# Cross-attention scores: float32 products in 32-row strips instead of stacked bf16 parts

## What is computed

```python
qh = layernorm(x).reshape(B, 8, 8, 256); kh = vh = ctx.reshape(B, 8, 8, 256)
qk = jnp.einsum('bhdq,bhdl->bhql', qh, kh) * 8 ** -0.5
sm = jax.nn.softmax(qk, axis=-1)
ret = jnp.einsum('bhql,bhdl->bhdq', sm, vh).reshape(B, 64, 256)
x = x + gamma * ret
# feed-forward on layernorm(x); bit_linear rounds its input to 8 bits per row, its weights to -1, 0, 1
h = silu(bit_linear(x, w_gate)) * bit_linear(x, w_up)
h = rms_norm(h, ln_weight)
x = x + bit_linear(h, w_down)
```

## Time and profile before

| what | before |
|---|---|
| time, median of 3 runs | 245.23 us (244.26 to 247.96) |
| span of the profiled execution | 248.6 us |
| PE busy, matrix products | 178.4 us (72%), 1370 records |
| DVE busy | 151.6 us (61%) |
| ACT busy | 140.9 us (57%) |
| POOL busy | 107.3 us (43%) |
| mean granted clock of PE | 0.89 of full |
| DMA | 19.95 MB in 15871 packets |

### The profile page before, as it was taken

How to read it: one execution, slowest core, us unless ns; L and a number is a source line. 1 busy time by engine, 2 the same in 40 slices (tenths; PEclk the granted TensorE clock), 3 DMA queues, 4 the chain that set the end, 5 groups by cost and what they waited for, 6 DMA issues and landing times.

```text
span 248.6 us, 4308 instructions
## 1 busy us (share of the span) xinstructions
PE 178.4 (72%) x1370; PEld 103.8 (42%) x1378; DVE 151.6 (61%) x282; ACT 140.9 (57%) x286; POOL 107.3 (43%) x282
## 2 busy tenths in 40 slices
PE   0006331972988958994999799589979998893793
PEld 0002111540666624662466366245745664441432
DVE  2105840563297974985666989736886769436273
ACT  4110000893466845973568599447856587975432
POOL 3630310406624544734652586436435226626240
PEclk9999999996599997997569999965995699999689
DMA  3599599348201450253026314601540000000000
GB/s 100 139 142 261 126 177 313 115 121 154 63 1 37 118 107 0 56 149 77 1 67 141 75 26 116 135 9 34 142 105 0 5 3 22 7 21 0 22 1 21
DMA packets 15871, 19.95 MB, mean 80 GB/s; under 512 B 2649, under 2 KB 14057, under 8 KB 14697
## 3 DMA queue, kind: packets, MB, share of 16 engines
q1 hardware_dynamic: 15321, 18.89, 31.8%
q10 hardware_dynamic: 528, 0.79, 1.4%
HBM read 15.20 MB, written 4.19 MB: 78 GB/s over the span
## 4 chain that ended last, share of the span: by engine, by line
PE 33%; DMA 14%; DVE 7%; issue 6%; ACT 6%; POOL 4%; SPq 3%; POOLq 0%; ACTq 0%; DVEq 0%
DMA q_stack<-mt 13%; PE psO L463 9%; PE psB L447 7%; PE psA L433 6%; PE psG L565 2%; PE psG L505 2%; ACT probs L594 2%; PE psG L555 2%; POOL hw L325 2%; DVE mneg L736 1%; SPq L333 1%; ACT o_sb L629 1%; SPq L341 1%; DVE wgT L755 1%; DVE w_sb L747 1%
## 5 line engine op out<-in xcount | busy, mean ns | idle before, releaser
L736 DVE TENSOR_REDUCE mneg<-psA 128x2 f32<-128x512 f32 x128 | 82.7, 680 | 46.5 <-PE psA L433 46.4
L594 ACT ACTIVATE probs<-psB 128x512 f32<-128x512 f32 x128 | 74.0, 597 | 39.8 <-PE psB L447 39.7
L433 PE MATMUL psA<-k_stack,q_stack 72*128 72x256 bf16 x256 | 57.9, 319 | 23.1 <-DMA q_stack<-q_scratch 20.7
L447 PE MATMUL psB<-q_stack,k_stack 75*128 75x256 bf16 x256 | 55.2, 303 | 23.8 <-DMA q_stack<-mt 22.0
L463 PE MATMUL psO<-probs,vt 128*32 128x256 f32 x512 | 41.6, 451 | 1.0 <-ACT probs L594 1.0
L433 PEld LDWEIGHTS psA<-k_stack,q_stack 72*128 72x128 bf16 x256 | 23.9, 108 | 43.3 <-issue 30.1
L447 PEld LDWEIGHTS psB<-q_stack,k_stack 75*128 75x128 bf16 x256 | 25.7, 108 | 37.2 <-DMA q_stack<-mt 23.8
L325 POOL TENSOR_TENSOR hw<-h,lnw 128x512 f32<-128x512 f32 x15 | 19.1, 1270 | 39.3 <-DVE h L826 28.0
L463 PEld LDWEIGHTS psO<-probs,vt 128*32 128x32 f32 x512 | 14.8, 121 | 16.9 <-issue 9.9
L815 DVE SCALAR_TENSOR_TENSOR gu<-th,psG 128x512 f32<-128x512 f32 x15 | 10.3, 688 | 9.7 <-ACT th L657 9.7
L657 ACT ACTIVATE th<-psG,tscale 128x512 f32<-128x512 f32 x15 | 10.3, 688 | 9.1 <-PE psG L535 9.0
(11 more groups left out here) (129 smaller groups left out, 268.4 us busy)
## 6 DMA issues: line engine op xcount, KB each, us to landing
q_stack<-q_scratch SPq DMA_DIRECT2D x24, 192.0 KB
k_stack<-k_scratch SPq DMA_DIRECT2D x21, 192.0 KB
q_scratch<-q_parts SPq DMA_DIRECT2D x24, 64.0 KB, 2.1
k_scratch<-k_parts SPq DMA_DIRECT2D x21, 64.0 KB, 2.0
w_sb<-in_L_ffn_w_gate_dram SPq DMA_DIRECT2D x4, 256.0 KB, 8.0
w_sb<-in_L_ffn_w_up_dram SPq DMA_DIRECT2D x4, 256.0 KB, 7.5
w_sb<-in_L_ffn_w_down_dram SPq DMA_DIRECT2D x4, 256.0 KB, 4.1
out_dram<-y_sb SPq DMA_DIRECT2D x8, 128.0 KB, 4.2
```

Of the source, the lines that this page charges most:

```text
L433: mm = pe.matmul(psA[n % A_BANKS][:, qt * L:(qt + 1) * L], q_stack[0:STACK, t % NBUF, bh, qt * P:(qt + 1) * P], k_stack[0:STACK, t % NBUF, ...
L447: mm = pe.matmul(psB[b % 2][:, lt * L:(lt + 1) * L], k_stack[:, t % NBUF, bh, lt * P:(lt + 1) * P], q_stack[:, t % NBUF, bh, :], start=Tru ...
L594: act.activation(probs[:, b % RING, :], psB[b % 2][:, :], ACT.Exp, scale=SCALE).then_inc(s_exp, 1)
L736: dve.tensor_reduce(mneg[:, k % MBUF, QT * (bh % HALF):QT * (bh % HALF + 1)], psA[n % A_BANKS][:, :].rearrange("p (q l) -> p q l", q=QT), ...
```

## The change

q and ctx stay float32 in SBUF. `q` holds, per tile, two copies of the normalised x, each with the rows of one half of the heads (the others multiplied by zero, `half_mask`). `cm` holds four copies of ctx, copy j with the rows of head j of each strip of 32 partitions only, zeros elsewhere, and ones in one row, against which the negated maxima stand in `q` in a row that is masked out there. So a unit's product runs over the 32 partitions of its strip, and only its 8 rows (and in the second scores the row of maxima) add anything. The scratch tensors, the split into parts and the stacks are gone. For tile 0 ACT makes `cm` from the loaded ctx; for the others the engines fill it with the ones and zeros (`clear_cm`), and 16 DMAs put ctx's rows in from DRAM.

The maxima are handed on per four units instead of eight, in float32: PE transposes `mneg` itself (8 x 128), ACT copies, SP sends. The second scores run 12 units behind the first. Weights are loaded by three DMAs from ACT's queue at the start.

```diff
-LAG = 14
+LAG = 12
-FIRST = -BH
+FIRST = -2
 def unit(n):
     t, i = divmod(n, BH)
-    return t, i, HALF * (i // HALF) + 2 * (i % GROUP) + (i % HALF) // GROUP
+    half, r = divmod(i, HALF)
+    return t, half, r, r // 2, 2 * (r % 2) + half
...
+        q = sb("q", [P, T, 2, L])
+        cm = sb("cm", [P, 4, T, L])
+        def one_row(j):
+            return STRIP // 2 * (j // 2) + DH * (1 - j % 2)
+        def clear_cm(eng, j):
+            return eng.tensor_scalar(cm[:, j, 1:T, :], zero[:, 0:1].unsqueeze(2).to_broadcast([P, T - 1, L]), mask[:, one_row(j):one_row(j) + 1], None, ALU.add)
...
         @block.sync
+            for j in (0, 2, 1, 3):
+                sp.wait_ge(s_init[j], 1)
+                for i in range(P // STRIP):
+                    rows = slice(STRIP * i + DH * j, STRIP * i + DH * (j + 1))
+                    sp.dma_start(cm[rows, j, 1:T, :], ctx_rows[1:T, rows].rearrange("g p l -> p g l")).then_inc(s_cm[j], DMA)
...
         @block.tensor
                 if not after and 0 <= n < N:
-                    t, i, bh = unit(n)
-                    if i == 0:
-                        pe.wait_ge(s_stack[t % NBUF], 2 * PARTS * DMA * (t // NBUF + 1))
+                    t, half, r, strip, j = unit(n)
+                    rows = slice(STRIP * strip, STRIP * (strip + 1))
...
-                        mm = pe.matmul(psA[n % A_BANKS][:, qt * L:(qt + 1) * L],
-                                       q_stack[0:STACK, t % NBUF, bh, qt * P:(qt + 1) * P],
-                                       k_stack[0:STACK, t % NBUF, bh, :], start=True, stop=True)
+                        mm = pe.matmul(psA[n % A_BANKS][:, qt * L:(qt + 1) * L], q[rows, t, half, qt * P:(qt + 1) * P],
+                                       cm[rows, j, t, :], start=True, stop=True)
...
-                        mm = pe.matmul(psB[b % 2][:, lt * L:(lt + 1) * L],
-                                       k_stack[:, t % NBUF, bh, lt * P:(lt + 1) * P],
-                                       q_stack[:, t % NBUF, bh, :], start=True, stop=True)
+                        mm = pe.matmul(psB[b % 2][:, lt * L:(lt + 1) * L], cm[rows, j, t, lt * P:(lt + 1) * P],
+                                       q[rows, t, half, :], start=True, stop=True)
...
-                    pe.transpose(banks[BANK_M][0:PARTS * HALF * QT, 0:P // 2].bitcast(BF16),
-                                 m_parts[:, k % 2].rearrange("p c n -> p (c n)"), ident_b[:, :]).then_inc(s_mt, 1)
+                    pe.wait_ge(s_red, GROUP * (k + 1))
+                    pe.transpose(banks[BANK_M][0:GROUP * QT, 0:P], mneg[:, k % MBUF, :], ident[:, :]).then_inc(s_mt, 1)
```

More of the change, by code:

```diff
@@ L222, in build @@
         s_rstd = sem("x_rstd")
[L223 to L231, removed]
+        s_q = sem("q_made")
         s_a = sem("a_scores")
         s_red = sem("row_max")
-        s_ms = sem("max_split")
         s_mt = sem("max_transposed")
@@ L336, in load_q @@
-        def load_q(eng, t):
-            eng.wait_ge(s_qst[t % 2], PARTS * DMA * (t // 2 + 1))
-            rows = q_scratch[t].rearrange("d c b l -> (d c) (b l)")
-            for c in range(PARTS):
-                eng.dma_start(q_stack[REP * c:REP * (c + 1), t % NBUF].rearrange("p b l -> p (b l)"),
-                              rows).then_inc(s_stack[t % NBUF], DMA)
-        def load_ones(eng, t):
-            eng.dma_start(k_stack[STACK:STACK_M, t],
-                          one_rows[:, :].unsqueeze(1).to_broadcast([PARTS, BH, L])).then_inc(s_ones[t], DMA)
@@ L371, in _ @@
[L371 to L394 removed]
+            sp.dma_start(x_sb[:, 0, :], x_rows[0]).then_inc(s_x[0], DMA)
@@ L395, in _ @@
+            for m in range(2 * FIRST, 2 * LAST):
+                k = quad_at(m, ACT_M)
                 if k is not None:
-                    t, half = divmod(k, 2)
+                    t, rest = divmod(k, 4)
+                    half, par = divmod(rest, 2)
+                    first = P // 2 * par + DH * (1 - half)
                     sp.wait_ge(s_mtsb, k + 1)
-                    sp.dma_start(q_stack[STACK:STACK_M, t % NBUF, half * HALF:(half + 1) * HALF, :]
-                                 .rearrange("c b (q l) -> c (b q) l", q=QT), mt[:, k % 2, :]).then_inc(s_mrow[half], DMA)
+                    sp.dma_start(q[first:first + P // 2 - DH:2 * DH, t, half, :].rearrange("p (q l) -> p q l", q=QT),
+                                 mt[:, k % 2, :]).then_inc(s_mrow[k % 2], DMA)
@@ L426, in _ @@
                 if not after and 0 <= n < N:
-                    t, i, bh = unit(n)
-                    if i == 0:
-                        pe.wait_ge(s_stack[t % NBUF], 2 * PARTS * DMA * (t // NBUF + 1))
+                    t, half, r, strip, j = unit(n)
+                    rows = slice(STRIP * strip, STRIP * (strip + 1))
+                    if r == 0:
+                        if t == 0:
+                            pe.wait_ge(s_q, half + 1)
+                            pe.wait_ge(s_cm0, 2 * (half + 1))
+                        else:
+                            pe.wait_ge(s_q, 2 * (t + 1))
+                            for jj in range(2):
+                                pe.wait_ge(s_cm[2 * jj + half], P // STRIP * DMA)
                     if n >= A_BANKS:
@@ L438, in _ @@
                 if after and 0 <= b < N:
-                    t, i, bh = unit(b)
-                    if i % HALF == 0:
-                        pe.wait_ge(s_mrow[i // HALF], DMA * (t + 1))
-                    if b < NBUF * BH and i == 0:
-                        pe.wait_ge(s_ones[t], DMA)
+                    t, half, r, strip, j = unit(b)
+                    rows = slice(STRIP * strip, STRIP * (strip + 1))
+                    if r % GROUP == 0:
+                        pe.wait_ge(s_mrow[r // GROUP], DMA * (2 * t + half + 1))
                     if b >= 2:
```

283 lines of the change are left out of this document (92 added, 191 removed).

## The result

The changed kernel takes 455.0 us (454.3 to 473.0) against 246.6 us of the kernel before beside it, a ratio of 1.858 (95% interval 1.847 to 1.869). Times in this document are medians of all executions, while a ratio with an interval uses only those within 1.5% of the fastest of their kernel. The clock was mostly at half, as the main case of the prediction had it; but the time lies under that case's 470 to 595 us, in the band from 400 to 470 us that had a chance of 0.10. The point of 525 us is 15% too high.

The account below looks back on a forecast made before the run. PE was taken as the bound: start 7, PE work 296.5 and tail 22.7 make 326 us at full clock, 587 at half; four fifths at half gives 535 in a profile, 525 us as forecast, range 322 to 595.

Parts of the forecast that it names:

- main case: Whole kernel: PE's clock mostly at half, 470 to 595 us, chance 0.50.
- the band from 400 to 470 us: Whole kernel: a time between the mostly-half range and that of a clock staying full, chance 0.10.
- rival 1: PE's clock: stays full because PE is never idle; 322 to 400 us, chance 0.30.
- four fifths of PE's work at half: PE's clock: 0.8 of the 261 us that hang on it added to 326, giving 535 us in a profile.
- The overlap: Score products on PE: only a block's last record runs beside the next's first, 121 places, 25 us back at full.
- rival 3: Score products: row strips have own queues, whole psA blocks run beside psB blocks; 238 us as a median, chance 0.04.
- the prediction's own sum: Whole kernel, start, PE's work and tail: 326 us all at full clock, 587 us all at half.
- Changes between strips and the whole array: PE's order: 247 changes, 32 already inside psO's time; 215 x 0.14 = 30 us.
- Start: Before the first product: 7 us (6 to 10) instead of 20.7.
- Maxima and tail: Six units, 9 us, before maxima are needed, so 22.0 us of waits go; 22.7 us behind the last psO group.

Follow-up runs that it names:

- e1: Changed kernel with both score products over all 128 rows instead of a strip's 32, maxima to a spare tile; 353.3 us in one run.
- e9: Changed kernel with score products over the 64 rows of the array half holding the unit's strip, maxima left out; 327.4 us.
- e8: Changed kernel with both score products reading only the high half of each float32 number as bf16; 288.9 us.
- e5: Changed kernel with the transposition of the maxima half a unit earlier, directly behind the psO group; 391.8 us.
- e10: Kernel before with maxima handed on per four units instead of eight, still bf16 parts, and POOL's split earlier; 278.7 us, ratio 1.146.
- e12: Kernel before with the DMA of the maxima issued by ACT instead of SP; 255.0 us, ratio 1.019.
- e4: Changed kernel with four masked copies of q and consecutive units in four different strips; 424.7 us.
- e6: The kernel of e4 with the transposition of the maxima directly behind psO, as in e5; 368.7 and 455.3 us.
- e2: Changed kernel with every unit's score products in strip 0, maxima to a spare tile; 660.8 us in one run.

## Why the prediction was right, and where its size was off

**Direction and cause: right.** The range of 322 to 595 us covers everything from all full to all half, so that the time fell into it says little; the windows, e1 and e9 are what bears out the cause. Float32 costs two records of 0.215 us per product (0.43 at half) as read from psO: the records in the timelines are that far apart, and e8 shows what it is worth. PE is the bound at over 90%.

**The clock: right in level, slightly too dark, and wrong about what lifts it.** The prediction gave "mostly half" 0.50, and 0.30 to a clock that stays full because PE is never idle. e1, e9 and after, with the same count of products and PE busy 91 to 94%, differ in the rows of the score products (and in what overlaps by them), and lie at full, at full and mostly at half. So rival 1 is refuted by the mechanism that the earlier trace rows suggested. The "four fifths of PE's work at half" was taken, not derived; that it came near is in part luck, since moving one transposition by half a unit (e5) already gives 392 us. Of the 1024 score records 265 lie in the windows at full (48, 46 and 14 of psA, 49, 46 and 62 of psB), so 759 ran at half, 74%.

The prediction expected psO groups, down projections and transposes to raise the clock. They did not: 14 psO groups lie in the two windows at half (80 and 144 records), while the 3.4 us ahead of each rise hold no psO record (0.00 us in each), and the clock fell at 168.9 and 267.9 us, some 4 us behind a down projection. The three rises, at 145.0, 244.0 and 401.0 us, come each within 2.2 us of the start of a stretch of four blocks abreast (143.35, 241.83, 399.24). Three more such stretches (182.67, 280.9, 340.07) had no rise behind them, so they are not enough by themselves; what else it needs stays open.

The Trainium skill, "TensorE: Matmul & The Clock Gate", section "Why this matters for your kernels", has the full clock follow from uninterrupted work; the window 168.9 to 244.0 us, busy for 75.10 of 75.10 us at 0.50, does not agree.

**The overlap: the step that failed.** "Records start in program order; only the last record of a block can run beside the first of the next" is wrong for row strips. Whole neighbouring blocks run side by side, up to four: 322 records beside an earlier one instead of 121, that is 201 x 0.215 = 43 us at full and 86 at half. It is the mechanism of rival 3, which had 0.04 and needed it for all blocks and at full clock throughout. The evidence I had against it, psO's records in their order, comes from column strips, which share all rows; it did not bear on row strips.

With this one term corrected the prediction's own sum gives 326 - 43 + 2 = 285 us all at full and 587 - 86 + 2 = 503 all at half (2 for the start, below). At 74% of the work at half, by the count of score records, that is 446 us. By time it is 433: the stretches at full last 92.2 us, 32% of 285, which leaves 68%. What the sum had at nothing comes on top: PE has 8.9 us without work between its first product and the last psO group (busy 410.64 of 419.56 us), and the tail is 1.2 us longer. That makes 443 to 456 us; the span is 452.7.

**Changes between strips and the whole array: the price a little high.** I took 0.14 us in and 0.14 out. Four records alone take 1.05 us at full instead of 0.86 (155.20 to 156.25), so in and out are 0.19 us together; at half 2.00 instead of 1.72 (189.35 to 191.35), 0.28. Their larger effect was not in the sum at all: a change ends the side-by-side running of the blocks around it.

**Start.** 9.2 us, not 7, inside 6 to 10. POOL's clear was sized by another POOL instruction (1.97 us for 2048 elements) and took 4.82 us for 1792; rstd behind it is late by that. Whether form or DVE beside it makes it slow is open for the first one, and a second at 12.55 us takes 4.84 us while DVE runs single reductions of 0.69 us, which speaks for the form.

**Maxima and tail.** The wait goes, as forecast (1.3 us once). That the rows had 9 us to arrive was not enough of a reason: e10 and e12 show that behind the stack loads they take over 7.5 us, and PE waited in both. The tail is 23.9 us from the end of the last psO group at 428.8 us on, forecast 22.7.

## What to carry to other kernels

A product in a 32-row strip took as long as one in the whole array (0.215 us a record in both), and with long runs of such work the clock stood at half; so more rows cost nothing here and even paid (e9: twice the rows, 128 us faster). A complete kernel of that kind would need twice as many masked copies, as two heads now share 64 rows; that was not tried. If strips are used, put consecutive blocks in different strips and gather all full-array work in one place, because each piece of it ends their running side by side (e4, e5: 91 and 67 more records beside another, e6 with both 158). And before moving an exchange earlier, look at what else is on the DMA engines when it is issued: a small transfer behind 1 MB took 7 to 8 us from either queue tried.

## What the runs showed of the hardware that was not expected

- Blocks in different row strips that follow each other in PE's list start together (0.01 us apart) and advance at 0.215 us a record each, against the list's order; blocks in one strip, and full-array products, do not. Up to four blocks in four strips run so. The Trainium skill, "TensorE: Matmul & The Clock Gate", section "The mechanism", has matrix products start and end in program order; the timeline from 149.80 us does not agree. The Trainium skill, "TensorEngine Tiling (Array Packing)", section "The Solution", calls the tiles of the array independent, and with that the timeline agrees.
- With PE busy throughout, the granted clock is 1.00 from 28.1 to 331.9 us with 128 rows, 1.00 from 99.7 to 307.9 us with 64, half for 351 of the 443 us from the first product on with 32, and for practically all of e2 with one strip.
- With 32-row strips the clock rose three times ahead of the tail, each time in a stretch of four blocks abreast or at its end, and directly behind none of 14 psO groups (the kernel after).
- Where no clock record lies ahead, the page shows full whatever the level was; the distance of the records in one strip tells it (0.215 or 0.43 us).
- Executions of one kernel whose clock changes its level often differ widely, e6 by 87 us.
- A transfer of 3 to 12 KB issued within a microsecond of six loads of 192 KB lands 7.2 to 7.8 us later, on their queue or on another.
